# Attention and mixture-of-experts block on one core: maxima turned behind the output, values in two half-slots, shifts ahead of the small steps

## The reference, cut to what matters

```python
# attention: 16 heads of 8, every query sees the last 64 positions
h = layernorm(x)
q, k, v = heads(h @ Wq), heads(h @ Wk), heads(h @ Wv)
scores = einsum(q, k_window) * 8 ** -0.5     # positions before 0: -inf
x = x + (softmax(scores) @ v_window) @ Wo
# experts: 8 experts of width 512, top 2, capacity 2048 slots each
h = layernorm(x)
w, e = top_k(softmax(h @ w_router), 2)       # w: the two gates, not renormalised
# pairs (token, expert) are put in order of expert; past the capacity they are dropped
y = gelu(slots @ w1[e]) @ w2[e]
x = x + sum(w * y) + bias
```

## Time and profile before

| | before |
|---|---|
| median of 3 runs | 877.89 us |
| the profiled execution | 880.53 us |
| its span, first to last instruction | 878.8 us |
| TensorE busy, matmuls | 747.0 us (85%) |
| TensorE busy, weight loads | 540.9 us (62%) |
| VectorE busy | 518.8 us (59%) |
| ScalarE busy | 452.3 us (51%) |
| GpSimd busy | 356.4 us (41%) |
| mean granted TensorE clock | 0.934 |
| first to last shift matmul (L1142) | 17.88 to 538.04 us |

### The profile page before, as it was taken

How to read it: one execution, slowest core, us unless ns; L and a number is a source line. 1 busy time by engine, 2 the same in 40 slices (tenths; PEclk the granted TensorE clock), 3 DMA queues, 4 the chain that set the end, 5 groups by cost and what they waited for, 6 DMA issues and landing times.

```text
span 878.8 us, 19093 instructions
## 1 busy us (share of the span) xinstructions
PE 747.0 (85%) x7425; PEld 540.9 (62%) x7425; DVE 518.8 (59%) x1592; ACT 452.3 (51%) x923; POOL 356.4 (41%) x318
## 2 busy tenths in 40 slices
PE   6999999999999999999999997205997988988970
PEld 3566666566566566566566664205997887887870
DVE  6887878978878888878878878401221211221110
ACT  5576685675676576576585563103452333333320
POOL 3000000024123123123123253660777777777877
PEclk9999999999999999999999998557999899999995
DMA  5941000001100101100100111113354544554533
GB/s 138 389 151 55 7 15 7 33 29 33 43 30 30 47 29 31 46 29 29 46 30 30 49 46 53 55 41 105 33 105 60 106 82 60 105 84 58 85 31 33
DMA packets 50130, 54.20 MB, mean 62 GB/s; under 512 B 6017, under 2 KB 39448, under 8 KB 49024
## 3 DMA queue, kind: packets, MB, share of 16 engines
q0 software_dynamic: 22528, 17.22, 13.5%
q1 hardware_dynamic: 27520, 35.86, 12.2%
HBM read 17.70 MB, written 31.59 MB: 56 GB/s over the span
## 4 chain that ended last, share of the span: by engine, by line
PE 36%; DVE 24%; issue 16%; POOL 15%; DMA 6%; another core or an unknown queue 1%; SPq 1%; POOLq 1%; ACT 0%; DVEq 0%; ACTq 0%
POOL out L444 14%; PE u_ps L1150 6%; PE sT_ps L1125 5%; DVE kmax L688 5%; PE sT_ps L1142 4%; DVE moving L702 3%; DMA out<-y_sb,xg 3%; PE o_ps L1159 3%; DVE negmax L694 2%; PE tail_ps L1165 2%; DVE negmax_hl L699 2%; PE tail_ps L1170 2%; PE o_ps L1134 2%; DMA x_sb<-in_L_attn_x 2%; DVE ctx_sb L714 2%
## 5 line engine op out<-in xcount | busy, mean ns | idle before, releaser
L444 POOL DMA_INDIRECT out<-y_sb,xg x128 | 198.8, 1553 | 81.5 <-DVE y_sb L1059 42.0
L363 POOL DMA_INDIRECT slots_dram<-send_rows,slot_id x112 | 110.1, 983 | 178.9 <-PE sT_ps L1142 134.5
L521 ACT ACTIVATE probsT<-sT_ps 128x1024 f32<-128x1024 f32 x128 | 132.1, 1032 | 62.4 <-PE sT_ps L1142 57.3
L688 DVE TRANSPOSE_TENSOR_REDUCE kmax<-sT_ps 128x32 f32<-128x1024 f32 x128 | 159.4, 1245 | 7.6 <-PE sT_ps L1125 7.1
L620 ACT ACTIVATE hT<-sT_ps 128x512 f32<-128x512 f32 x128 | 76.6, 598 | 143.9 <-PE sT_ps L1354 114.2
L1125 PE MATMUL sT_ps<-qbd,kT 64*128 64x256 f32 x1024 | 133.2, 380 | 0.0
L378 POOL TENSOR_TENSOR xbias<-x_sb,bias_sb 128x256 f32<-128x256 f32 x32 | 23.4, 732 | 246.3 <-PE sT_ps L1142 246.3
L1354 PE MATMUL sT_ps<-xT_hl,w_hl 128*128 128x512 f32 x384 | 103.8, 423 | 18.3 <-DVE xT_hl L1046 18.3
L1125 PEld LDWEIGHTS sT_ps<-qbd,kT 64*128 64x128 f32 x1024 | 98.5, 191 | 9.8
L1354 PEld LDWEIGHTS sT_ps<-xT_hl,w_hl 128*128 128x128 f32 x384 | 75.0, 202 | 35.2 <-issue 13.1
L1046 DVE TENSOR_TENSOR xT_hl<-u_ps,xT_hl 128x512 fp32r<-128x512 f32 x32 | 22.1, 690 | 109.0 <-ACT xT_hl L613 105.9
(11 more groups left out here) (171 smaller groups left out, 1130.0 us busy)
## 6 DMA issues: line engine op xcount, KB each, us to landing
slots_dram<-empty_rows SPq DMA_DIRECT2D x8, 1096.0 KB, 16.5
xg<-slots_dram SPq DMA_DIRECT2D x32, 274.0 KB, 3.5
out<-xbias SPq DMA_DIRECT2D x32, 128.0 KB
w_sb<-in_L_ffn_w SPq DMA_DIRECT2D x16, 256.0 KB
send_rows<-rows_sb SPq DMA_DIRECT2D x7, 548.0 KB, 3.2
out<-y_sb,xg POOLq DMA_INDIRECT x128
slots_dram<-send_rows,slot_id POOLq DMA_INDIRECT x112
out<-empty_rows SPq DMA_DIRECT2D x1, 1024.0 KB, 24.8
```

Source lines behind the costliest of these rows:

```text
L363: pool.indirect_dma_start(out=slots_dram, out_offset=bass.IndirectOffsetOnAxis(ap=slots[:, k, j:j + 1].bitcast(U32), axis=0), in_=rows[:, ...
L444: pool.indirect_dma_start(out=out, out_offset=bass.IndirectOffsetOnAxis(ap=xg[:, r, 4 * c + k, ROW - 1:ROW].bitcast(U32), axis=0), in_=y_s ...
L521: nc.scalar.activation(probsT[:, gp].rearrange("p b k h q -> p (b k h q)"), sT_ps[:, gp].rearrange("p b c -> p (b c)"), ACT.Exp).then_inc( ...
L688: nc.vector.tensor_reduce(kmax[:, u % 2, :], sT_ps[:, u % 2].rearrange("p b (c q) -> p (b c) q", q=32), AX.X, ALU.max, apply_transpose=Tru ...
```

## The change

Nothing is computed differently. On TensorE `maxima_T(2g+1)` comes directly behind `project`, ahead of `query_key`; `normed_T` goes behind the first `fill` of the slot, with a wait for the values of the pair before. `values` does one tile at a time: the first behind the slot's second `fill` with odd t, the second ahead of the first `fill` in the slot after it. On ScalarE the keys' copies go behind the second `exps`, and `values` has three copies per tile in place of four per pair, the second tile's ahead of the copy of the transposes. On VectorE `stats_ahead` (but for t = 2) and `shifts(2g+1)` come ahead of `small`, `residual`, the logits and `positions`.

```diff
@@ ScalarE
-            def query_key(n, p, bank=proj_ps):
+            def queries(n, p, bank=proj_ps):
...
+            def keys(n, p, bank=proj_ps):
                 for gp in range(2):
...
-            def values(n, p, bank=proj_ps):
-                act.wait_ge(s_v, n + 1)
...
-                put(slice(0, P), slice(0, P), p, 1, 2, 0)
-                put(high, low, p, 0, 2, 0)
-                put(low, high, p, 2, 1, 0)
-                put(low, high, (p + 1) % PAIRS, 0, 1, 1).then_inc(s_v_sb, 1)
+            def values(n, p, tile, bank=proj_ps):
+                act.wait_ge(s_v, 2 * n + tile + 1)
                 low, high = slice(0, BLK), slice(BLK, P)
+                ring, after = (p, 2) if tile == 0 else ((p + 1) % PAIRS, 0)
+                for out_rows, rows, at, place in ((slice(0, P), slice(0, P), p, 2 * tile + 1), (high, low, p, 2 * tile),
+                                                  (low, high, ring, after)):
+                    last = nc.scalar.activation(v_sb[out_rows, at, place, :, 0:2 * DH],
+                                                bank[rows, tile * P:(tile + 1) * P].rearrange("p (j c) -> p j c", c=2 * DH),
+                                                ACT.Copy)
+                last.then_inc(s_v_sb, 1)
@@ ScalarE, slot
                 if not (first and t == 0):
                     weighted_out(g - 1)
+                if t % 2 == 0 and not (first and t == 0):
+                    values(b * PAIRS + t // 2, t // 2 % PAIRS, 1)
                 if t % 2 == 0 and (t < 4 or not last):
                     normed_T(b * PAIRS + (t + 4) // 2, (t + 4) // 2 % PAIRS)
                 if t % 2 == 1 and (t < 5 or not last):
-                    query_key(b * PAIRS + (t + 3) // 2, (t + 3) // 2 % PAIRS)
+                    queries(b * PAIRS + (t + 3) // 2, (t + 3) // 2 % PAIRS)
...
                 exps(g, 1)
+                if t % 2 == 1 and (t < 5 or not last):
+                    keys(b * PAIRS + (t + 3) // 2, (t + 3) // 2 % PAIRS)
...
                 if t % 2 == 1 and (t < 7 or not last):
-                    values(b * PAIRS + (t + 1) // 2, (t + 1) // 2 % PAIRS)
+                    values(b * PAIRS + (t + 1) // 2, (t + 1) // 2 % PAIRS, 0)
@@ VectorE, slot
                 part_max(2 * g + 1)
                 gap(b, t, 0, chain, first)
+                if t != 2:
+                    stats_ahead(b, t, first)
+                shifts(2 * g + 1)
                 small(b, t, 0, chain, route, old_route, first, last)
-                stats_ahead(b, t, first)
+                if t == 2:
+                    stats_ahead(b, t, first)
...
-                shifts(2 * g + 1)
                 if ahead:
                     part_max(2 * g + 2)
@@ TensorE
-            def values(n, p, bank=proj_ps):
-                for s in range(2):
+            def values(n, p, tiles, bank=proj_ps):
+                for s in tiles:
                     at = BLK + (2 * p + s) * P
-                    last = mm(bank[:, s * P:(s + 1) * P], xnT[:, at:at + P], wv_sb[:, :], start=True, stop=True)
-                last.then_inc(s_v, 1)
+                    mm(bank[:, s * P:(s + 1) * P], xnT[:, at:at + P], wv_sb[:, :], start=True, stop=True).then_inc(s_v, 1)
@@ TensorE, slot
                     project(g - 2)
-                if t % 2 == 1 and (t < 5 or not last):
-                    query_key(b * PAIRS + (t + 3) // 2, (t + 3) // 2 % PAIRS)
-                if t % 2 == 0 and (t < 4 or not last):
-                    n = b * PAIRS + (t + 4) // 2
-                    pe.wait_ge(s_v_sb, n - 1)
-                    pe.wait_ge(s_k_sb, n)
-                    normed_T(n, (t + 4) // 2 % PAIRS)
...
                 maxima_T(2 * g + 1)
+                if t % 2 == 1 and (t < 5 or not last):
+                    query_key(b * PAIRS + (t + 3) // 2, (t + 3) // 2 % PAIRS)
+                if t % 2 == 0 and not (first and t == 0):
+                    n = b * PAIRS + t // 2
+                    pe.wait_ge(s_v_sb, 2 * n + 1)
+                    values(n, t // 2 % PAIRS, (1,))
                 pe.wait_ge(s_exp, 2 * g + 1)
                 if ahead:
...
                     fill((t + 1) % TILES, 0)
+                if t % 2 == 0 and (t < 4 or not last):
+                    n = b * PAIRS + (t + 4) // 2
+                    pe.wait_ge(s_v_sb, 2 * (n - 1))
+                    pe.wait_ge(s_k_sb, n)
+                    normed_T(n, (t + 4) // 2 % PAIRS)
...
                 shifted(2 * g + 1)
-                if t % 2 == 0:
-                    pe.wait_ge(s_v_sb, b * PAIRS + t // 2 + 1)
+                pe.wait_ge(s_v_sb, 2 * (b * PAIRS + t // 2) + t % 2 + 1)
...
                 if ahead:
                     maxima_T(2 * g + 2)
+                if ahead:
+                    pe.wait_ge(s_exp, 2 * g + 2)
+                    fill((t + 1) % TILES, 1)
                 if t % 2 == 1 and (t < 7 or not last):
                     n = b * PAIRS + (t + 1) // 2
                     if t < 5 or not last:
                         pe.wait_ge(s_k_sb, n + 2)
-                    values(n, (t + 1) // 2 % PAIRS)
-                if ahead:
-                    pe.wait_ge(s_exp, 2 * g + 2)
-                    fill((t + 1) % TILES, 1)
+                    values(n, (t + 1) // 2 % PAIRS, (0,))
```

More of the change, by code:

```diff
@@ L586, in _ @@
             act.wait_ge(c_dve, 1)
-            query_key(0, 0)
+            queries(0, 0)
+            keys(0, 0)
             act.wait_ge(c_dve, 2)
             act.wait_ge(c_ones, 1)
-            values(0, 0, o_ps)
+            act.wait_ge(s_v, 2)
+            values(0, 0, 0, o_ps)
+            values(0, 0, 1, o_ps)
             normed(1)
             normed_T(1, 1, u_ps)
-            query_key(1, 1, u_ps)
+            queries(1, 1, u_ps)
+            keys(1, 1, u_ps)
             normed(2)
@@ L1295, in _ @@
             query_key(0, 0)
-            values(0, 0, o_ps)
+            values(0, 0, (0, 1), o_ps)
             fill_zeros(5)
```

4 lines of the change are left out of this document (removed).

## The result

The changed kernel takes 892.58 us in the median of 4 runs (891.25 to 896.99), the kernel before 877.84 us beside it (877.73 to 878.0): a ratio of 1.0177, with an interval of 1.014 to 1.0213. It is slower by some 15 us, where +2.1 was forecast and 886 was the upper end of the range. The execution profiled is the 891.25 one, with a span of 889.5 us.

The account below looks back on a forecast made before the run. TensorE was taken as nearly the bound in attention (busy 62.47 of 66.21 us per sequence). Slot gains and losses summed to +0.2 in the fifth sequence and +2.1 over all, 877.9 to 880.0 us; range 871 to 886.

Parts of the forecast that it names:

- The first sequence: First eight attention slots, which have no routing: forecast to change by -1.4 us.
- the forecast itself: Whole kernel: +2.1 us on the 877.9 median, 880.0; chance 0.50, with its own range 877 to 884.
- Maxima's turn behind project: Every slot: turn at S+1.22, reduce at S+1.71, R released at S+3.02; the second shift's wait goes in plain slots.
- TensorE's own row: TensorE's work becomes next late: odd first half 3.98 to 3.72, even 3.33 to 3.39; plain pair about -0.5 us.
- Values in halves: TensorE: 0.64 becomes 0.32 in each slot of a pair; odd second half 4.25 to 3.94, even stays 3.81.
- VectorE's shifts ahead: VectorE's small steps follow the shifts and delay the next big maximum: t = 2 +0.72, t = 0 +0.17, t = 6 +0.39.
- the named chain: t = 4: row copies start late on ScalarE, delaying second exponentials and the fill behind them; 8.03 to 8.85, +0.82.
- Rival A: Faster: ScalarE's order in t = 4 does not hold; 873.6, or 864 with VectorE's slots also unbounded; chance 0.30.
- Rival C: Nothing: waits merely change place and VectorE's total sets the pace; 877.9, +/- 1; chance 0.08.
- Rival B: Slower: the new t = 4 hole before the router's slots tips TensorE's clock, 1.33 x 7 = 9: 889; chance 0.12.
- Unknown prices: VectorE's bf16 cast beside GpSimd scatter issues takes 0.47 or 0.18; bounds -4 to +10 us, taken as 0.

Follow-up runs that it names:

- the turn alone: Kernel before with only `maxima_T(2g+1)` moved directly behind `project`: 878.33 us, 1.0006; the same in all slots but t = 5: 876.26 us, 0.9941.
- moving the rows: Changed kernel with both `normed_again` calls of t = 4 put behind ScalarE's second exponentials: 888.82 us, 1.018.
- both causes mended: Changed kernel with `normed` of t = 3 ahead of values, t = 4 row copies behind second exponentials, t = 4 `normed` in t = 5, VectorE's old order: 876.22 us, 0.9987.
- ScalarE is mended: Changed kernel with `normed` of t = 3 ahead of values, t = 4 row copies behind second exponentials, `normed` of t = 4 in t = 5: 883.63 us, 1.0059.

## Why the prediction was wrong

The sum came out at +0.2 us per sequence where it was +2.1. The chains that it followed are there in the traces; what failed are terms of it. In t = 4 project's wait for ScalarE was put at nothing (0.56 us with what hangs on it). In t = 6 the slow cast was put at nothing (0.28) and the rest came 0.19 short. In t = 0 the sum lacks 0.60, of which 0.45 is the late release that three of the experiments do not have. The first sequence was put at -1.4 and came at +0.78. That the time rose is little credit: slower had a chance of 0.39, and the forecast itself was hardly to be told from no change.

- **Maxima's turn behind project: right.** The waits of second shifts fell from 55 to 1, the reduce started at S+1.81 (forecast 1.71), and the turn alone, where t = 5 is spared, is worth 0.6% (shown).
- **TensorE's own row: mis-sized.** The forecast of a plain pair was 3.39 + 3.81 + 3.72 + 3.94 = 14.86, measured 15.16. The step that failed here is 0.64 becoming twice 0.32: one tile alone takes 0.42 from start to start in front of the fill. Two changes of operand that were reckoned at the old distances cost 0.09 and 0.06 more. A pair gained 0.22 instead of 0.51, which is 1.2 us per sequence where no other bound stands. The first sequence was forecast at -1.4 and came at +0.78. It has no routing, but its t = 2 and 4 are not plain: t = 2 grew by 1.05, of which VectorE's old order gives back 0.84, and t = 4 by 1.08, of which `normed` ahead of the values gives back 0.77. The forecast priced neither there.
- **Values in halves: right place, wrong reason.** They were reckoned as TensorE's term. In one piece they cost another 1% through ScalarE (shown). That they gain anything is not shown: with them and both causes mended the ratio is 0.9987, without them and with the early turn alone 0.9941.
- **VectorE's shifts ahead: right mechanism, mis-sized.** t = 1, 2, 3 and 7 came within 0.2 of the sums. t = 0 and 6 came at +0.77 and +0.86 where +0.17 and +0.39 were put; taking the order out gives 0.45 and 0.79 of that back, but the 0.45 is the late release described above, which comes and goes with either order. In t = 6 the big maximum starts at S+4.99 where S+4.71 was forecast; that 0.28 is a cast that takes 0.46 instead of 0.18. Taking the order out gives back up to 12 of the attention's 14.8 us, and 7.9 where ScalarE is mended already; in the forecast its slots lost 1.28 and won 1.57, for it was credited with wins in t = 1, 3 and 7 that come from TensorE's edits. With the old order and the new turn these slots are just as fast (8.24, 7.89 and 8.04 us).
- **t = 4: the named chain was right**, +0.82 by it and 8.85 measured once project's wait is gone (the rows then start at S+4.02, forecast 3.97). The match to the hundredth is partly luck: the transposes start 0.17 later than forecast, and the copy follows them 0.13 sooner. Project's wait, 0.50, is the missed term: `normed` in t = 3 stands in front of the context's copy, with ScalarE busy 8.64 of 9.41 us in t = 4. The step "what is late next" was followed to the fill and not back to project.
- **Rival A** (ScalarE's order would not hold) is refuted: it holds, and moving the rows gave 1.07 in t = 4. **Rival C** (the waits change place and the time stays) is half right: they did change place, at a price of 15 us.
- **Rival B** (the clock): the mechanism exists and is not this loss. Behind the first slot the attention stage has none to four falls in a profile, 23 in the 13 traces, and all of them begin 1.6 to 2.4 us into a t = 6, where the last of the router's 8-column matmuls starts at 1.7. The kernel after had none in one profile and two in the other, at ratios of 1.0177 and 1.0192. The Trainium skill, TensorE: Matmul & The Clock Gate, "What's actually happening", has activity as what lifts the clock. By that rule the new hole in t = 4 makes a fall there likelier; the rows above show 1.00 in that slot, no trace has a fall in any t = 4, and one falls to 0.50 in a microsecond in which TensorE is busy for all of it.
- **Unknown prices: taken at 0, right in the count and wrong in the place.** The bf16 cast is slow (over 0.3 us) 10 times in 128 in the trace of before, 9 times after, never with VectorE's old order in the changed kernel (but 5 times where ScalarE is mended as well). The extra time sums to 3.0 us before and 2.4 after. But before it falls into t = 5, which TensorE bounds, and t = 7; after, into t = 6, where VectorE's row is the late one, and into the late t = 0. The Trainium skill, GPSIMD Engine Reference, section 1 (Specifications), tells of interfaces shared by GpSimd and VectorE. The traces agree that VectorE is held up beside scatter issues, at some of them only; the last section has the condition.
- **The range** reached 886 from the port's and the clock's price. It had no term for several slots being late together by small amounts, which is what happened: +1.9 per sequence over eight slots, of which three hold 1.63.

What stays open: why the big maximum is released 0.4 us late in t = 0 in one kernel and not in another with the same instructions around it, and in some sequences of a kernel only; and what starts the falls of the clock. The 2.8 us that the rest of the kernel is shorter in the trace after is not the change's: what follows the last shift takes 341.9 us in the second profile of the same changed kernel, 338.3 with the turn alone, and 338.0 to 343.6 over all traces.

## What to carry to other kernels

An instruction moved ahead on one engine has to find its input ready at the new place: count the idle time it will stand in front of, in every slot, and what is queued behind it that used to fill that time. A gain on the bound engine's wait is only worth having where a second engine does not become late from the same move, so each moved edit is best run alone: here one moved line holds all of the gain (0.9941), and the whole change stands some 2.4% above it. Where a wait is counted by line, take the places on that line apart before you call it mended or not. Split a piece of work by the measured price of a piece, not by half the price of the whole.

## What was not expected of the hardware

- The values of one tile (one float32 matmul in the code, two instructions in the trace) take 0.42 us from start to the start of the fill behind them, those of two tiles (four instructions) 0.64: the third and fourth cost 0.22 together, the first two nearly twice that. The turn behind project stands 0.42 behind it, the transposes of before 0.33 behind it.
- TensorE's granted clock can fall to 0.50 (1.2 GHz) while the engine is busy for the whole time, and come back by itself. Of the 23 falls in t = 6, 19 last about 3 us and 4 twice that; the slots are longer by 0.35 to 2.7 us. In 11 of the 13 traces it falls in the first slot too, there behind a stretch with little TensorE work (1.6 of the 4.5 us in the kernel before), and the first two slots take 17.4 to 17.8 us with it and 17.5 without (18.6 in the one trace where it lasts twice as long). The number of falls differs from one profile of a kernel to the next. The runs of one kernel spread by up to 8 us, and the longer ones tend to have the lower mean clock: with the turn alone 881.54 us at 0.925 and 874.45 at 0.935. That goes with the falls, but the traces do not show that it is all of the spread.
- A bf16 cast of 0.18 us on VectorE (L704) takes up to 0.47 in some places and never in others. The kernel after, t = 6 of the fifth sequence:

```profile
339.44 0.98 POOL L363 DMA_INDIRECT slots_dram<-send_rows,slot_id  x1 [0.30 <-issue]
...
339.97 0.46 DVE L704 CAST negmax_hi<-negmax 128x32 bf16<-128x32 f32 x1
```

The cast starts 0.53 into GpSimd's issue of a scatter and ends with it. All 13 traces have 96 casts that start 0.52 to 0.75 into such an issue: 94 of them end within 0.01 us behind its end, whatever their start, so they take 0.47 to 0.23. The other two stand in an issue that is 1.17 us long instead of 0.98, and take 0.18. Of the casts that start in its first 0.49 us none takes more than 0.21. So a cast is slow by where it starts, and an edit that shifts it by 0.1 us can bring or remove up to 0.29. This was read from the traces; no run moved a cast or an issue to test it.
